# A fused transformer block on one core: q, k, v and the first FFN matmul computed as three float32r products

## What is computed

```
mod = (silu(c) @ wmod).reshape(8, 6, 1, 256);  sa, ca, ga, sb, cb, gb = mod[:, 0..5]
h = layernorm(x) * (1 + ca) + sa
q, k, v = [h @ w.T + (h @ a.T @ b.T) / 16 for w, a, b in ...]      # split into 16 heads of 16
attn = softmax(where(causal, q @ k.T / 4, -inf))
x = x + ga * lora_linear(attn @ v, wo, ao, bo)
h = layernorm(x) * (1 + cb) + sb
w = top 2 of softmax(h @ Wg.T + bg);  hid_e = relu(h @ Wi.T + h @ A_e.T @ B_e.T)
x = x + gb * sum_e w_e * (hid_e @ Wo.T)
```

## Time and profile before

| | us |
|---|---|
| median of 3 runs | 1978.09 (1977.63 to 1978.61) |
| profiled execution | 1980.25 |
| its span, first to last instruction | 1978.5 |
| TensorE busy | 1802.2 (91%) |
| VectorE busy | 1234.0 (62%) |
| ScalarE busy | 941.8 (48%) |
| GpSimd busy | 532.9 (27%) |
| mean granted clock of TensorE | 0.973 |

### The profile page before, as it was taken

The page is one execution under the profiler, slowest core; times in us unless marked ns, Lnnn a source line. Parts: engine busy times, 40 slices in busy tenths (PEclk is TensorE's granted clock), DMA queues, the critical chain, the costliest instruction groups (busy, mean ns, idle before and its releaser), DMA issues.

```text
span 1978.5 us, 31549 instructions
## 1 busy us (share of the span) xinstructions
PE 1802.2 (91%) x10868; PEld 942.1 (48%) x10868; DVE 1234.0 (62%) x2681; ACT 941.8 (48%) x1701; POOL 532.9 (27%) x833
## 2 busy tenths in 40 slices
PE   7698889999989999999989999899999999899868
PEld 5343344454544555454644545444554545344535
DVE  3676577657676567756686577766677555753131
ACT  2255465544555455544455445544455444544320
POOL 2112122322313222233223222133222232133223
PEclk9789899999999999999999999999999999899979
DMA  7613432313321313223323223213222222220000
GB/s 179 146 54 91 82 82 55 76 42 75 74 80 39 94 44 81 68 41 76 85 60 71 52 67 85 67 41 92 60 47 66 45 76 57 39 42 23 25 0 22
DMA packets 249862, 128.69 MB, mean 65 GB/s; under 512 B 158214, under 2 KB 244834, under 8 KB 249708
## 3 DMA queue, kind: packets, MB, share of 16 engines
q1 hardware_dynamic: 245564, 125.61, 26.4%
q10 hardware_dynamic: 4144, 1.07, 0.4%
HBM read 83.06 MB, written 41.97 MB: 63 GB/s over the span
## 4 chain that ended last, share of the span: by engine, by line
PE 71%; DVE 17%; ACT 5%; issue 3%; SPq 2%; DMA 2%; POOL 0%; POOLq 0%; DVEq 0%; ACTq 0%
PE dense L855 11%; PE ov L911 11%; PE st L896 10%; PE mxs L880 8%; PE dense L998 6%; PE dense L936 5%; PE dense L841 5%; PE dense L849 4%; DVE negm L1311 4%; DVE negm_left L1311 3%; PE dense L861 3%; PE mxs L884 2%; PE dense L928 2%; ACT probs L1046 2%; SPq L651 2%
## 5 line engine op out<-in xcount | busy, mean ns | idle before, releaser
L1046 ACT ACTIVATE probs<-st 128x512 f32<-128x512 f32 (+1 forms) x1216 | 672.6, 576 | 717.6 <-PE st L896 715.1
L1311 DVE TENSOR_REDUCE negm<-mxs 128x1 f32<-128x384 f32 (+4 forms) x736 | 444.9, 617 | 258.0 <-PE mxs L884 255.3
L896 PE MATMUL st<-q_st,k_st 98*128 98x512 bf16 (+3 forms) x1536 | 451.8, 332 | 24.8 <-ACT probs L1046 17.4
L880 PE MATMUL mxs<-k_st,q_st 96*128 96x512 bf16 (+3 forms) x1280 | 401.3, 324 | 34.9 <-DVE negm_left L1311 20.8
L1311 DVE TENSOR_REDUCE negm_left<-mxs 128x1 f32<-128x512 f32 x512 | 343.1, 687 | 141.7 <-PE mxs L880 140.6
L911 PE MATMUL ov<-probs,v_g 128*32 128x512 f32 (+3 forms) x3072 | 332.0, 505 | 1.4 <-POOL probs L743 1.4
L855 PE MATMUL dense<-c_t,wi_t 128*128 128x512 f32 x512 | 266.3, 606 | 12.3 <-DVE second L1365 11.6
L880 PEld LDWEIGHTS mxs<-k_st,q_st 96*128 96x128 bf16 x1280 | 123.4, 98 | 269.9 <-issue 103.4
L756 POOL TENSOR_TENSOR hid<-hid,second 128x512 f32<-128x512 f32 x128 | 161.8, 1266 | 305.3 <-DVE second L1365 305.3
L896 PEld LDWEIGHTS st<-q_st,k_st 98*128 98x128 bf16 x1536 | 142.4, 99 | 169.6 <-ACT probs L1046 71.0
L740 POOL TENSOR_TENSOR fence<-fence 128x1 f32<-128x1 f32 x256 | 51.5, 201 | 621.8 <-ACT probs L1046 621.8
(11 more groups left out here) (165 smaller groups left out, 1700.8 us busy)
## 6 DMA issues: line engine op xcount, KB each, us to landing
q_st<-q_parts_scratch SPq DMA_DIRECT2D x384, 64.0 KB
k_st<-k_parts_scratch SPq DMA_DIRECT2D x384, 64.0 KB
q_parts_scratch<-q_part SPq DMA_DIRECT2D x16, 768.0 KB, 3.3
k_parts_scratch<-k_part SPq DMA_DIRECT2D x16, 768.0 KB, 5.2
xin<-in_L_attn_x SPq DMA_DIRECT2D x8, 1024.0 KB, 5.8
values_scratch<-v_rows SPq DMA_DIRECT2D x32, 256.0 KB, 2.1
v_g<-values_scratch SPq DMA_DIRECT2D x128, 64.0 KB, 3.9
x<-in_L_attn_x SPq DMA_DIRECT2D x16, 512.0 KB, 4.3
```

Source lines behind the costliest of these rows:

```text
L880: last = nc.tensor.matmul(mxs[:, bank_m, j * n:j * n + left], q_st[0:KS, slot, h0 + j, qt * P:(qt + 1) * P], k_st[0:KS, slot, h0 + j, k0:k ...
L896: last = nc.tensor.matmul(st[:, score_bank(ch, kt, h0), j * n:(j + 1) * n], k_st[0:KS + 2, slot, h0 + j, kt * P:(kt + 1) * P], q_st[0:KS + ...
L1046: nc.scalar.activation(probs[:, par, h0:h0 + heads, 0:n], st[:, score_bank(ch, kt, h0), 0:heads * n].rearrange("p (j q) -> p j q", q=n), A ...
L1311: nc.vector.tensor_reduce(dst[:, h0:h0 + heads], src, axis=AX.X, op=ALU.max, negate=True).then_inc(max_free, 1)
```

## The change

**Products.** Each float32 product of q, k, v and the first FFN matmul becomes three float32r products: high times high, high times low, low times high. The weights' parts are made once in the setup, the high part by ScalarE's copy into a float32r tile, the low one by VectorE. h is split once per batch: VectorE copies it (`hs`, four copies of 128x512) and GpSimd subtracts (`hl`, four). c, the input of the FFN, is split by GpSimd alone (`ch`, four copies; `cs`, four subtractions, after `rt` has read c). The output projection and the second FFN matmul stay float32.

**Order.** The applications of the second norm (`ln2`, parts 3 to 6) go from VectorE to GpSimd. All eight tiles of q and k go behind unit 20, between the FFN's tiles, which begin at unit 21, not 17. v's four steps go from units 7, 8, 12, 13 to 7, 9, 11, 14. t2 goes from unit 10 to 12, `rt` from 11 to 13, the routing from 12 to 14 to 14 to 19, `ps` from 17 and 36 to 25 and 38, the load of the next x from 3 to 31. The parts of q and k have one buffer in place of two, so a tile's copy by ScalarE waits until both earlier `ps` DMAs have landed. Low parts share the memory of h and c.

```diff
-            "pa": 875, "pj": 875, "va": 875, "vp": 875, "fa": 875, "fx": 1095, "fb": 220, "wa": 875, "w": 875,
+            "pa": 640, "pj": 640, "va": 680, "vp": 680, "fa": 640, "fx": 860, "fb": 220, "wa": 875, "w": 875,
...
-        for i, u in enumerate((7, 8, 8, 8, 9, 9, 9)):
+        for i, u in enumerate((9, 9, 9, 10, 10, 11, 11)):
             chains[u].append(("ln2", i))
-        slots[10] += [("t2", i) for i in range(4)]
-        slots[11] += [("rt",), ("rx",)]
...
+        slots[12] += [("t2", i) for i in range(4)]
+        if pre:
+            for half in range(2):
+                chains[half].append(("hs", half))
+            for i in range(4):
+                begins[3 + i].append(("hl", i))
+        for i in range(4):
+            begins[14 + i].append(("ch", i))
+            begins[16 + i].append(("cs", i))
+        slots[13] += [("rt",), ("rx",)]
...
-            slots[17 + 30 * i // len(dense)] += q
+            slots[21 + 26 * i // len(dense)] += q
...
-PJ_UNITS = (0, 6, 10, 11, 15)
-PJ_SLOTS = (5, 9, 13)
-V_UNITS = (7, 8, 12, 13)
-PS_UNITS = (17, 36)
+PJ_UNITS = ()
+PJ_SLOTS = (0, 1, 2, 3, 9, 10, 11, 12)
+V_UNITS = (7, 9, 11, 14)
+PS_UNITS = (25, 38)
...
+                elif kind == "hl":
...
+                    pool.wait_ge(h_high, of_half(KC * done("hs"), half))
+                    nc.gpsimd.tensor_tensor(h_lo[:, k, cols], h_t[:, k, cols], h_hi[it >= 0][:, half, k, :].bitcast(F32),
+                                            ALU.subtract).then_inc(h_split, 1)
+                elif kind == "ln2" and a[0] >= 3:
+                    pool.wait_ge(norm_chain, (done("normed") + 1) * NORM_LINKS)
+                    for t in range(2 * a[0] - 6, 2 * a[0] - 4):
+                        last = nc.gpsimd.tensor_scalar(x2n[:, t, :], x1[:, t, :], nt[:, 1, t:t + 1],
+                                                       nt[:, 3, t:t + 1], ALU.mult, ALU.add)
+                    last.then_inc(norm2_ready, 1)
...
+                        nc.gpsimd.tensor_copy(c_hi[:, k, cols], c_t[:, k, cols]).then_inc(c_high, 1)
+                    else:
+                        pool.wait_ge(dense_full, done("rt full"))
...
-                return nc.tensor.matmul(db[:, :], w_t[:, WNAMES.index(which), k, ot * P:(ot + 1) * P],
-                                        h_t[:, k, half * HB:(half + 1) * HB], start=(k == 0), stop=(k == KC - 1))
+                for i, (w, h) in enumerate(((w_hi, high), (w_hi, low), (w_lo, high))):
+                    last = nc.tensor.matmul(db[:, :], w[:, m, k, cols], h, start=(k == 0 and i == 0),
+                                            stop=(k == KC - 1 and i == 2))
...
+                    for j, (h, w) in enumerate(((high, w_hi), (high, w_lo), (low, w_hi))):
+                        last = nc.tensor.matmul(db[:, n * D:(n + 1) * D], h, w[:, 2, k, :],
+                                                start=(k == 0 and j == 0), stop=(k == KC - 1 and j == 2))
...
+                for i, (w, c) in enumerate(((wi_t, c_hi), (wi_t, c_lo), (wi_lo, c_hi))):
+                    nc.tensor.matmul(db[:, :], w[:, k, rows], c[:, k, cols], start=(k == 0 and i == 0), stop=False)
...
                     elif kind == "pa":
-                        project(db, 0, *a)
+                        pe.wait_ge(h_split, of_half(done("hl"), a[2]))
+                        project(db, 0, *a, it)
...
                     elif kind == "fa":
+                        pe.wait_ge(c_split, of_half(done("cs"), a[0]))
                         hidden(db, 0, *a)
...
-                    after(act, parts_out[ot], done(f"ps{ot}") * (2 * 16))
+                    for i in range(2):
+                        after(act, parts_out[i], done(f"ps{i}") * (2 * 16))
...
+                elif kind == "hs":
...
+                    for k in range(KC):
+                        nc.vector.tensor_copy(h_hi[it >= 0][:, half, k, :], h_t[:, k, half * HB:(half + 1) * HB]
+                                              ).then_inc(h_high, 1)
```

218 lines of the change are left out of this document (144 added, 74 removed).

## The result

The changed kernel takes 2024.28 us (median of 4 runs, 2021.63 to 2024.91) against 1977.86 us for the kernel before in the same comparison (1977.39 to 1978.61): 1.0234 times as long, interval 1.0222 to 1.0246. The forecast was 1915 us and its range ended at 1957. The change is slower by 46 us where 63 us were to be gained.

What follows compares the result with a forecast made beforehand. The prediction took TensorE to bound the kernel (busy 1802.2 of 1978.5 us). Six middle batches 9 us shorter each, setup +3.5, first batch -1.5, last -6.5, tail -5 gave 1915 us, range 1866 to 1957.

Steps and rivals of the forecast that it cites:

- The product: A float32r product of 512 columns takes 0.22 us, three 0.65 against 0.86 now; saves TensorE 11.5 us per batch.
- v's loads: Weight loads of v's products stay hidden beside the matmuls; in series they would add 5.3 us per batch.
- rival (c): Slower: a float32r product costs 0.43 us, three 1.29; 24 us more per batch, 2170 us in all; chance 0.07.
- Rival (a): TensorE's waits in the middle batches go as well: 212 us each, 17 less, 1867 us in all; chance 0.17.
- The second part gets 18.6 us and gives back 3.3 and 6.6.: Units 21 to 47 of a middle batch: TensorE busy 134.3 us instead of 125.6, taking 138 us.
- The first part is no longer TensorE's.: Units 0 to 20 of a middle batch: TensorE falls from 90.6 to 70 us; they take 77 to 85, taken as 82.
- It costs nothing as long as the causal mask isn't late.: GpSimd's added 18 us per batch put at nothing, with 3 us per batch as bound if masks come late.
- Rival (b), the light part stalls: Units 9 to 11 and 15 to 20 leave TensorE idle, clock falls: 226 us per batch, 1951 in all; chance 0.17.
- Setup, +3.5: Before the first unit: exposed split of h and maxima sharing VectorE add 1 to 5.6 us, taken as +3.5.
- First and last batch: First batch 1.5 us shorter, its VectorE as full as before; last batch 6.5 shorter, by the FFN alone.
- Tail, -5: After the last batch: 16 FFN tiles save 6.6 us, norm on GpSimd gives 1.6 back; 5 us shorter.
- Moved DMAs, nothing: First parts of q and k sent at unit 25, next overwritten in unit 28, over 10 us later; no cost.

Runs made afterwards that it cites:

- e5: Changed kernel with each score product issued twice in units 12 to 20 of the six middle batches: 2019.14 us.
- e12: Changed kernel with four q/k tiles in units 10, 12, 13, 16, FFN from unit 22, setup reordered with earlier norm, second norm on VectorE: 1964.25 us.
- e11: Kernel before, with half of the depth of the q, k and v projections left out in the batches: 1955.33 us.
- e9: Changed kernel with second norm, routing and FFN start back near the units of the kernel before; new products, split and setup kept: 2012.76 us.
- e3: Changed kernel with GpSimd's split of c cut to one column instead of 512 from the third batch on: 1989.40 us.
- e4: Changed kernel with setup reordered: second-half q/k tiles ahead of the first maxima, six weight transposes between the maxima: 2008.35 us.
- e8: Changed kernel with thin units refilled, setup reordered with earlier norm, high part of c from ScalarE, second norm on VectorE: 1997.89 us.

## Why the prediction was wrong, point by point

- **The product.** Right in kind, 9% off in size: 0.235 us instead of 0.215 or 0.22 for 512 columns, 0.117 for 256. Three cost 0.70, not 0.65. A tile of 512 columns saves 0.31 us instead of 0.42, a batch some 9 instead of 11.5, eight batches some 20 us less than reckoned. v's loads stay hidden, and rival (c) fell. Rival (a) fell too: TensorE's waits in a middle batch didn't go, they grew from 12.6 to 19.4 us.
- **"The second part gets 18.6 us and gives back 3.3 and 6.6."** Reckoned 138 us, measured 148.1. Busy time is 139.5 instead of 134.3: about 2.6 us are the products' price (144 at 0.018), some of the rest the stretch at 1.2 GHz. And the wait beyond busy is 8.6 us, not 3.7. This step holds most of the miss: 10.6 of the 13.1 us per batch. The largest term that was missing is the collision of unit 21, 5.1 us longer than before for 1 us more of products. I read the moved transposes as 1.8 us of TensorE's work, and not as two 1.0 us copies of ScalarE that hold both banks beside the maxima's row. e5 puts 1.7 us of it on the clock's fall in that unit. e12, which moves the tiles of q and k off unit 21, gets 4.1 us per batch more out of the second part than they weigh; its units 21 and 22 are 1.8 us shorter with no fewer products in them. The other waits of this part (0.6 to 1.5 us each in units 24, 25, 38 and 45) no run takes apart.
- **"The first part is no longer TensorE's."** Right, and 83.9 us lies in 77 to 85, but partly by luck: 4.6 us of it are a cost that I had put at nothing (the next point). I also took the 97.9 us of before as TensorE's, with gaps. e11 shows that in 42.9 of them, units 7 to 15, most of what is taken off TensorE buys nothing: of 6.0 us none was gained, and some 2.5 would be at full clock. e9, which puts norm and routing back into the units of before, ends where before was, with less work for TensorE. Both fit a first part that shortened mainly because VectorE's norm and routing were stretched over more units. They don't prove it, since both runs also brought 12 to 15 us at 1.2 GHz into each first part; a run that holds the clock up with the order of before would be needed.
- **"It costs nothing as long as the causal mask isn't late."** Wrong. The price of GpSimd's work was paid by VectorE, not by the masks, for which TensorE waited 1.4 us in the whole run, as before. By e3 the split of c costs 4.6 us of each middle batch in units 0 to 20, 5.0 with the second part, and 2.7 us of the tail's routing wait. I looked for who waits for GpSimd and not for who shares something with it.
- **Rival (b), the light part stalls.** This came true in its signs, a clock below 1.00 in every middle batch, but I gave it 226 us per batch and measured are 229.8 to 235.1. It had no share for what GpSimd takes from VectorE or for unit 21.
- **Setup, +3.5.** Measured +24.3: 6.4 for the norm behind the weights' low parts, 4.6 for the split of h against 3.5 reckoned, 11.2 for the tiles between the maxima, 2.1 elsewhere. I counted what is added and not what the single part buffer forbids; e4 and e8 give 17.9 of the 24.3 back by order alone, with the same single buffer.
- **First and last batch.** Forecast -1.5 and -6.5, measured -3.6 and -4.8.
- **Tail, -5.** Measured +3.3. An FFN pair of tiles repeats every 4.53 us instead of 5.14, 4.9 us in eight. Against that stand 2.7 us of routing wait, 0.8 of norm wait, and the clock: the output projection's 32 products take 9.02 us instead of 7.17, and 1.2 GHz lasts until 1957.7, into the FFN. The same tail took 115.6 to 117.7 us in five other runs, with 31 to 38 us at 1.2 GHz instead of 44; so 3 to 5 us of the miss go with this one execution's clock, and the tail as such gained next to nothing on the 117.1 of before.
- **Moved DMAs, nothing.** Nothing in these runs speaks against it; it was not tried alone.

Sum of what was missed, forecast to span: setup 21, middle batches 79 (13.1 each), last batch 2, tail 8, less 2 for the first batch, is 108 us: 1915 becomes 2023. Of a middle batch's 13.1 us, 5.0 are GpSimd's split (e3), 2.8 the products' price, and 1.7 the clock in unit 21 (e5), if these can be added; the last 3.6 stay open.
